# A fused graph and transformer kernel: the written-out order of all queues is redrawn, and the copies of transposed attention weights are shared out evenly between two engines

## The chip, the cores and the metric

The kernel runs on one core of a Trainium2 chip. The metric is device microseconds of one execution. A core has four compute engines with queues of their own (TensorE, called PE in the profile; VectorE, DVE; ScalarE, ACT; GpSimd, POOL) and SyncE (SP), whose queue issues the DMAs here. Each engine takes its instructions strictly in the order of its queue and waits on semaphores for the others.

## The reference

`x` is 16 graphs of 512 nodes with 128 features, `adj` a 512 x 512 integer adjacency for each. Eight blocks are added to `x` one after another, each on a layer norm of what stands before it:

```
x = x + L0_gnn(layernorm(x), adj)   # 3 steps of messages and a GRU cell
x = x + L0_ffn(layernorm(x))        # 8 experts, top 2, gelu
x = x + L1_gnn(layernorm(x), adj)   # graph attention: leaky relu, softmax, elu
x = x + L1_ffn(layernorm(x))        # attention over 64 slices, 8 heads
x = x + L2_gnn(layernorm(x), adj)   # mean of messages
x = x + L2_ffn(layernorm(x))        # Mamba-2 block, chunks of 128
x = x + L3_gnn(layernorm(x), adj)   # two layers of masked attention, 4 heads of 32
x = x + L3_ffn(layernorm(x))        # upper half of tokens through an FFN
```

The part that the change edits is one layer of L3_gnn, for 4 tiles of 128 queries and 4 heads:

```
scores = where(adj > 0, q @ k.T * scale, -1e9)
attn = softmax(scores); out = attn @ v
```

## The kernel before, in words

In the code the eight blocks are g0, f0, g1, f1 (the early half) and g2, f2, g3, f3 (the late half). Matrices are tiled by 128 partitions, T = 4 tiles of 128 nodes. Two graphs are in flight at any time, in two sets of buffers ("lanes"): while graph h goes through its early half, graph h-1 goes through its late half. `halves` (line 396) builds each engine's queue from this: a first phase (graph 0 early, alone), 15 equal periods in which an early and a late half run beside one another, and a last phase (graph 15 late, alone).

Every block is a Python generator that stops at each place where its instructions may be interrupted. A string for each engine (PE_TURNS, ACT_TURNS, DVE_TURNS, POOL_TURNS, SP_TURNS) says whose piece comes next: `e` is the early graph's, `l` the late graph's. The same string serves all 15 periods. PE_FIRST, DVE_FIRST and ACT_FIRST do so for the first phase, PE_LAST for TensorE's last phase; the other engines take their natural order there.

TensorE's strings hold one more kind of turn. A digit (in the periods) or a `w` (in the first and last phase) is a pair of products of the bf16 identity with itself, whose result nobody reads, in a PSUM bank that is free at that point: the "constant products" (`keep`, line 1056, and `keep_bank`, line 1060). They wait for nothing. PE_TURNS of the kernel before has 138 such turns in 28 runs, PE_FIRST has 378, PE_LAST 517.

In g3, each (layer, query tile q, head h), numbered n = 4q + h from 0 to 15 in a layer, goes through this chain:

- TensorE `g3_scores` (line 878): the scores of 4 heads into PSUM.
- VectorE `g3_mask` (line 1860): masks and takes the maximum.
- ScalarE `g3_exp`, then VectorE `g3_sum` (line 1867): exponential and reciprocal of the sum.
- GpSimd `g3_normalise` (line 2089): multiplies by it.
- TensorE `g3_turn` (line 903): four 128 x 128 transposes into PSUM bank 4 (later ones by turns into bank 0); before them it waits until the copy before has emptied the bank.
- `g3_turned`: the copy from PSUM to SBUF. VectorE makes it for head 0 (n % 4 == 0, line 1877), ScalarE for heads 1 to 3.
- TensorE `g3_values`: after 8 of these copies, the product with v.

All of ScalarE's activations are recorded at line 1068, all of TensorE's plain products at line 444, and to_columns (the transposes of a layer-normed tile) at line 453. In stage B below, ScalarE makes the gelu of f0 for the early graph and the exponentials of g3 for the late one; the two functions lie in different activation tables, and a change of table is an ACT_TABLE_LOAD instruction.

Of the kernel before, what the change touches and what calls it, by code (L numbers as in the profile page):

```python
# [28 lines left out]
T = N // P  # L29
# [9 lines left out]
AH, AD = 4, 32  # L39
# [38 lines left out]
    "lleele"  # L78
)
PE_FIRST = (  # L80
    "eewwwwwweeeeeeeeeewwwwwwwwwwwwwwwwwwwwwwwwwwwwwwwwweeeeeeeeeewwwwwwwwwwwwwwwwwwwwwwwwwwwwwwwwweeeeee"
    "eeeewwwwwwwwwwwwwwwwwwwwwwwwwwwwwwwwweppeeeewwwwwwwwweeeeeeeeeeeeeeeeeeeeeeeeeeeeeeeeeeeeeeeeeeeewww"
    "wwwwwwwweeeeewwwwwwwwwwwwwwwwwwwwwwwwwwwwwwwwwwweeeewwwwwweeewwwwwwwwwwwwwwwwwwwwwwwwwwwwwwwwwwweeww"
    "wwwwwewwwwwewwwwwweeeewwwwwwwwwwwwwwwwwwwwwwwwwwwwwwwwwwweeeewwwwwwewwwwewwwwwwwwwwwwwwwwwwweewwwwwe"
    "wwwwwwwwwwwwwwwwwwwwwwewwwwwwweeeeewwwwwwwwwwwwwwwwwwwwwwwwewwwwwwwewwwwwweewwwwwwwwwwwwewwwwwwewwww"
    "wweeee"
# [3 lines left out]
    "wwwwwwwwwlllwwlwlllllllwwwwwwwwwwwwwwwwwwwwwwwwwwwwwwwwwwwlllllllwwwlwwwwwwwwwwwwwwwwwwwwwwwwwllllww"  # L90
    "wwwwwwwwwwwwwwwwwwwwwwwwwwwwwwwwwllllwwwwwwllllwwwwwwwwwwwwwlwwwwwwwwwwwwwwwwwwwwwwwwwwwwllwwwwwwwww"
    "lwwwwwwwwwwwwlllwwwwwwwlwwwwwwwwlwwwwwwwwwwwwlllwwwwwwllllwwwwlwwwwwwwwlwwwwwwwwwwwwllwwwlwwwwwllwwl"
    "wwwwwwllllwllllwwwwwwwwwwwwwlwwwwwwwwwwwwwwwwwwwwwwwwwwwwllwwwwwwwwwlwwwwwwwwwwwwlllwwwwwwwlwwwwwwww"
    "lwwwwwwwwwwwwlllwwwwwwllllwwwwlwwwwwwwwlwwwwwwwwwwwwllwwwlwwwwwllwwlwwwwwwllllwwwllllwwwwwwwwwwwwwww"
    "wwwwwwwwwwwwwwwwwwwwllllwwwwwwllllwwwwwwwl"
# [8 lines left out]
    "ee7777eelellll7777lllllleeeeeeellll7777lllleleeleeeeeellell7lllllll11eeeeeeeeellellll77l7l7777777777"  # L104
    "7e777777777777lllleeee777777eee777777777lleelleelllleeleeee7777leeelleeeeellleleele33333llllllleeeel"
    "eeeeleeeeeeeeeeell44eellelleellll33lleleeeleee7l7777777777777777777eele77e777777leeeel1111lll11111l1"
    "1111111111l11eeeelellellllel111111lellel44ll4lelllleeeeelllle77777e77777ellllelellelelllelee"
)
ACT_TURNS = (
    "eellleeelellllllleellllleleelellleeeeleeeeeelleelllleelllllllllllllleeelelleeleelllllllleleeeeeeelee"  # L110
    "eelleellllllelllllelllelelelellllllelelleleeeeleellll"
)
DVE_TURNS = (
    "ellllelllllllelllleeeeellllllllelllleelllllleelelllllellellelleeelleeeeellleleeleeeeeeleellelllllell"
    "llllellllllllllelleleleellleeeeeeelleeeeellllellllllleeleleleellellleeleeeeleeellellleeelleeeeeeelle"
    "llelleeleellleeeellelle"
)
POOL_TURNS = (
    "llelellellllllllllllllllllellllllleleelllellllleelle"
# [27 lines left out]
def build(nc, x, adj, weights, raw, out):  # L147
# [10 lines left out]
    with ctx:  # L158
# [93 lines left out]
        with nc.Block() as block:  # L252
# [84 lines left out]
            "att_p": 2 * T * AH, "pT_psum": 2 * T * AH, "pT_dve": 2 * T, "pT_act": 2 * T * (AH - 1), "pv_psum": 4, "h3_part": 4,  # L337
# [24 lines left out]
        def turned(layer, n, g):  # L362
            if n % AH == 0:
                return done("pT_dve", g, layer * T + n // AH)
            return done("pT_act", g, (layer * T + n // AH) * (AH - 1) + n % AH - 1)
# [46 lines left out]
        with nc.Block() as block:  # L412
# [29 lines left out]
            def _(pe):  # L442
# [463 lines left out]
                def g3_values(g, layer, pair):  # L906

                    yield
                    pe.wait_ge(*turned(layer, AH * (2 * pair + 1), g))
# [156 lines left out]
            def _(act):  # L1066
# [262 lines left out]
                def g3(g):  # L1329
                    yield from columns_out(g, G3)  # L1330
                    for layer in range(2):
                        yield from g3_project(g, layer)
                        for n in range(T * AH + AH):
                            if n < T * AH:
                                yield from g3_exp(g, layer, n)
                            if n > AH and n % AH:
                                yield from g3_turned(g, layer, n - AH)
# [17 lines left out]
            def _(v):  # L1355
# [636 lines left out]
                def g3(g):  # L1992
                    yield from layernorm(g, G3, X[g])
                    for layer in range(2):
                        yield from g3_project(g, layer)
                        for q in range(T + 1):
# [4 lines left out]
                            if q < T:  # L2001
                                for h in range(1, AH):
                                    yield from g3_mask(g, layer, q * AH + h)
# [211 lines left out]
```

## Time and profile before

| what | value |
|---|---|
| median of 3 runs | 3431.71 us (3428.83 to 3431.92) |
| profiled execution, its own time | 3433.32 us |
| its span in the trace | 3431.5 us |
| mean granted TensorE clock | 0.994 |
| TensorE busy | 3231.9 us, 94% |
| VectorE busy | 2208.7 us, 64% |
| ScalarE busy | 1752.7 us, 51% |
| GpSimd busy | 693.3 us, 20% |

The span is from the first to the last instruction of the trace; the execution's own time also holds what lies around it. Busy time of TensorE counts the constant products as well.

### The profile page before, as it was taken

To read this page: it belongs to the slowest core of one execution; us is meant where nothing else is said; L and a number is where in the kernel's file an instruction comes from. 1 tells how busy PE (TensorE), PEld (TensorE's weight loads), DVE (VectorE), ACT (ScalarE), POOL (GpSimd) and SP (SyncE) were. 2 spreads that over 40 slices of the span, in tenths; PEclk is the share of its full clock that TensorE was granted. 3 is DMA by queue.
4 is the path that set the end of the run, shared out by engine and by line. 5 is a ranking of instruction groups with operands and counts; after the bars stand their busy time and mean duration, and the time that the engine had idled before them with its cause. 6 is when DMAs were issued, how large, how long until landed. Compare 5 with 4: busy or idle time off the path is not lost.

```text
span 3431.5 us, 62674 instructions
## 1 busy us (share of the span) xinstructions
PE 3231.9 (94%) x24744; PEld 2268.1 (66%) x24776; DVE 2208.7 (64%) x7062; ACT 1752.7 (51%) x3195; POOL 693.3 (20%) x804
## 2 busy tenths in 40 slices
PE   8999999999999999999999999999999999999989
PEld 5766666666666666666666666666666666666677
DVE  3476666757567676666757567676666757566653
ACT  2237454563645537454563645537454563645524
POOL 0012122121221212122121221212122121221212
PEclk9999999999999999999999999999999999999999
DMA  3000000000000000000000000000000000000000
GB/s 132 2 7 1 20 4 17 7 1 20 4 17 7 1 22 1 19 4 17 7 1 19 4 17 7 1 22 1 19 4 17 7 1 19 1 4 4 1 8 5
DMA packets 28773, 40.68 MB, mean 12 GB/s; under 512 B 1344, under 2 KB 17728, under 8 KB 28224
## 3 DMA queue, kind: packets, MB, share of 16 engines
q1 hardware_dynamic: 28480, 36.67, 3.4%
q8 instruction: 197, 3.23, 0.4%
q14 instruction: 96, 0.79, 0.1%
HBM read 28.28 MB, written 4.19 MB: 9 GB/s over the span
## 4 chain that ended last, share of the span: by engine, by line
PE 56%; DVE 26%; ACT 11%; issue 5%; POOL 2%; DVEq 0%
PE ps L444 45%; ACT scratch L1068 8%; DVE scratch L1359 5%; PE ps L903 4%; DVE scratch L1362 4%; DVE scratch L1365 3%; DVE scratch L1860 3%; PE ps L453 2%; DVE x L1365 2%; PE ps L1056 2%; DVE stats L1380 2%; POOL rstd L2066 1%; ACT adjf L1068 1%; DVE xn L1362 1%; ACT xT L1068 1%
## 5 line engine op out<-in xcount | busy, mean ns | idle before, releaser
L1068 ACT ACTIVATE scratch<-scratch 128x512 f32<-128x512 f32 (+4 forms) x832 | 564.8, 691 | 278.9 <-DVE scratch L1359 128.9
L444 PE MATMUL ps<-xT,weights_sb 128*128 128x512 f32 x1152 | 560.9, 604 | 7.9 <-ACT xT L1068 7.8
L444 PE MATMUL ps<-scratch 128*128 128x128 f32 (+6 forms) x4608 | 534.4, 379 | 35.7 <-ACT adjf L1068 14.1
L2089 POOL TENSOR_SCALAR scratch<-scratch 128x512 f32<-128x512 f32 x512 | 352.6, 703 | 933.0 <-DVE scratch L1867 932.3
L1068 ACT ACTIVATE scratch<-ps 128x512 f32<-128x512 f32 (+2 forms) x512 | 286.5, 566 | 426.2 <-PE ps L444 230.7
L444 PE MATMUL ps<-weights_sb,scratch 128*128 128x128 f32 (+3 forms) x3840 | 492.6, 278 | 5.9 <-DVE scratch L1503 5.9
L444 PEld LDWEIGHTS ps<-weights_sb,scratch 128*128 128x128 f32 (+3 forms) x3840 | 442.2, 184 | 56.8 <-issue 29.2
L444 PEld LDWEIGHTS ps<-scratch 128*128 128x128 f32 (+5 forms) x4608 | 341.4, 159 | 174.2 <-issue 92.1
L903 PE MATMUL ps<-weights_sb,scratch 128*128 128x128 f32 x2048 | 307.0, 279 | 61.4 <-ACT adjf L1068 24.6
L2066 POOL TENSOR_TENSOR rstd<-ve,minus_half 128x4 f32<-128x4 f32 x126 | 142.9, 1134 | 1081.0 <-DVE ve L1362 1081.0
L1860 DVE CUSTOM_DVE_ANT_0 scratch<-ps,nomask 128x512 f32<-128x512 f32 x512 | 332.7, 683 | 10.5 <-PE ps L444 10.2
L444 PEld LDWEIGHTS ps<-xT,weights_sb 128*128 128x128 f32 x1152 | 197.9, 190 | 212.8 <-issue 145.0
L903 PEld LDWEIGHTS ps<-weights_sb,scratch 128*128 128x128 f32 x2048 | 222.3, 141 | 170.9 <-issue 104.2
L1060 PE MATMUL ps<-ident_bf 128*128 128x128 bf16 x4140 | 300.4, 219 | 0.0
L1068 ACT ACTIVATE scratch<-ps,weights_sb 128x512 f32<-128x512 f32 x368 | 244.8, 686 | 88.5 <-PE ps L444 87.7
L1060 PEld LDWEIGHTS ps<-ident_bf 128*128 128x128 bf16 x4140 | 264.4, 99 | 34.1 <-issue 29.4
L1068 ACT ACTIVATE scratch<-ps,made_sb 128x512 f32<-128x512 f32 x176 | 120.4, 684 | 301.2 <-PE ps L444 301.0
L1068 ACT ACT_TABLE_LOAD x202 | 259.2, 1283 | 18.2 <-PEq L252 14.7
L1068 ACT ACTIVATE xT<-ps 128x512 f32<-128x512 f32 x112 | 66.9, 597 | 342.4 <-PE ps L453 342.4
L444 PE MATMUL ps<-adjf,scratch 128*32 128x256 f32 (+1 forms) x1280 | 241.6, 425 | 0.0
L1365 DVE SCALAR_TENSOR_TENSOR x<-ps,scratch,x 128x128 f32<-128x128 f32 x576 | 161.8, 344 | 111.5 <-PE ps L444 93.6
L1068 ACT ACTIVATE adjf<-ps 128x512 f32<-128x512 f32 (+1 forms) x288 | 166.3, 577 | 89.5 <-PE ps L903 67.2
(166 smaller groups left out, 4520.1 us busy)
## 6 DMA issues: line engine op xcount, KB each, us to landing
adj<-adj SPq DMA_DIRECT2D x16, 1024.0 KB, 5.7
weights_sb<-weights SPq DMA_DIRECT2D x1, 4605.0 KB, 19.0
x_in<-x SPq DMA_DIRECT2D x16, 256.0 KB, 2.8
scratch<-scratch SPq DMA_DIRECT2D x32, 128.0 KB, 2.3
out<-x SPq DMA_DIRECT2D x16, 256.0 KB, 2.4
scratch<-raw SPq DMA_DIRECT2D x1, 1645.0 KB, 22.4
weights_sb<-weights SPq DMA_DIRECT2D x1, 499.0 KB, 6.5
scratch<-raw SPq DMA_DIRECT2D x1, 384.0 KB, 4.9
```

What stands on the lines that cost most here:

```text
L444: return pe.matmul(o, lhsT, rhs, start=start, stop=stop, **k)
L453: last = pe.transpose((ep if k < G2 else lp)(0, P, P, t * P), rows[:, t, 0:D], ident)
L903: last = pe.transpose(lp(turn_bank(n), P, P, j * P), probabilities(g, layer, n)[:, tile(j)], ident)
L1056: pe.matmul(ep(0, P) if h else lp(3, P, P, 384), ident_bf[:, :], ident_bf[:, :], start=True, stop=True)
L1060: pe.matmul(banks[k][0:P, 0:P], ident_bf[:, :], ident_bf[:, :], start=True, stop=True)
L1068: return act.activation(o, a, func, **k)
L1359: return v.tensor_tensor(o, a, c, op)
L1362: return v.tensor_scalar(o, a, s1, s2, op0, op1, **k)
L1365: return v.scalar_tensor_tensor(out=o, in0=a, scalar=s1, in1=c, op0=op0, op1=op1, **k)
L1860: v.tensor_tensor_reduce(probabilities(g, layer, n), lp(n % AH), NM[g][:, n // AH, :], -1.0, 4 * BIG, ALU.add, ALU.min, cut(g, G3_MX + n, ...
L2066: pool.tensor_tensor(rstd[g][:, :], ve[g][:, :], minus_half[:, :], ALU.pow).then_inc(s[f"rstd_ready{g % LANES}"], 1)
L2089: pool.tensor_scalar(p, p, cut(g, G3_RI + n, 1), 1.0, ALU.mult, ALU.mult).then_inc(s["att_p"], 1)
```

## The change

The change has three parts.

1. Who copies. `g3_turned` is made by VectorE for even n (heads 0 and 2) and by ScalarE for odd n (heads 1 and 3). Of the 32 copies of a graph, 8 go from ScalarE to VectorE. In VectorE's queue the new copy of head 2 of tile q - 1 stands after the masks of tile q and before the reciprocals of tile q. `turned` and the semaphore counts follow.
2. The order. PE_TURNS, ACT_TURNS, DVE_TURNS, POOL_TURNS and SP_TURNS are new strings.
3. The constant products. PE_TURNS has 124 turns of them in 26 runs, PE_FIRST 376, PE_LAST 537.

The edits of the code:

```diff
         def turned(layer, n, g):
-            if n % AH == 0:
-                return done("pT_dve", g, layer * T + n // AH)
-            return done("pT_act", g, (layer * T + n // AH) * (AH - 1) + n % AH - 1)
+            return done("pT_act" if n % 2 else "pT_dve", g, (layer * T * AH + n) // 2)
...
                 def g3_values(g, layer, pair):
                     yield
-                    pe.wait_ge(*turned(layer, AH * (2 * pair + 1), g))
+                    pe.wait_ge(*turned(layer, AH * (2 * pair + 2) - 2, g))
                     pe.wait_ge(*turned(layer, AH * (2 * pair + 2) - 1, g))
...
# ScalarE's g3
-                            if n > AH and n % AH:
+                            if n > AH and n % 2:
                                 yield from g3_turned(g, layer, n - AH)
...
# VectorE's g3
                             if q < T:
                                 for h in range(1, AH):
                                     yield from g3_mask(g, layer, q * AH + h)
+                            if q:
+                                yield from g3_turned(g, layer, (q - 1) * AH + 2)
+                            if q < T:
                                 for p in range(2 * q, 2 * q + 2):
                                     yield from g3_sum(g, layer, p)
```

The new order of TensorE and SyncE (VectorE's, ScalarE's and GpSimd's strings are redrawn in the same way):

```diff
 SP_TURNS = (
-    "lleele"
+    "elleel"
 PE_TURNS = (
-    "ee7777eelellll7777lllllleeeeeeellll7777lllleleeleeeeeellell7lllllll11eeeeeeeeellellll77l7l7777777777"
-    "7e777777777777lllleeee777777eee777777777lleelleelllleeleeee7777leeelleeeeellleleele33333llllllleeeel"
-    "eeeeleeeeeeeeeeell44eellelleellll33lleleeleeee7l7777777777777777777eele77e777777leeeel1111lll11111l1"
-    "1111111111l11eeeelellellllel111111lellel44ll4lelllleeeeelllle77777e77777ellllelellelelllelee"
+    "ele7777ee77777llllelllllleeeeeeellll7777llllelleeeeeelelllellllelll222222eeeeelllellllleeeelllle7777"
+    "7777777777777777777777777777777777eeeellllelllleel7eeeeeeeeel7eleeeeeeeleeeeeeeleeeeelleeeleeeleelll"
+    "eeelllleleleeleel4llll66666llleeeeleeelllelee7l7e7777e7l7leeel33333ll222l22222l22222l333333333ll2l22"
+    "222lllle3leee333lelelll6666lleellllelllle77777eeeellllelleleleellle77777eleeee"
```

## Rows read from the trace of the kernel before

The stages of the period from 1207.3 to 1413.1 us are: A, to 1281.4 (g0 beside g2 and f2); B, to 1331.0 (f0 beside layer 0 of g3); C, to 1384.0 (g1 and the start of f1 beside layer 1 of g3); D, to 1413.1 (the end of f1 beside f3).

**Rows 1.** The page: busy us of the engines; group of the constant products.
```profile
...
PE 3231.9 (94%) x24744; PEld 2268.1 (66%) x24776; DVE 2208.7 (64%) x7062; ACT 1752.7 (51%) x3195; POOL 693.3 (20%) x804
...
L1060 PE MATMUL ps<-ident_bf 128*128 128x128 bf16 x4140 | 300.4, 219 | 0.0
...
```

**Rows 2.** Windows (first phase, a period, last): us, busy PE PEld DVE ACT POOL, clock.
```profile
...
0.00:178.00 178.00, 161.38 (x1328) 121.67 (x1331) 77.82 (x244) 42.85 (x70) 13.51 (x16) 0.92 0.17 64
1207.30:1413.10 205.80, 194.74 (x1448) 134.97 (x1450) 137.22 (x440) 109.88 (x200) 43.46 (x50) 1.00 0.04 10
3265.40:3431.50 166.10, 149.91 (x1698) 122.27 (x1698) 77.61 (x260) 62.86 (x126) 29.88 (x40) 0.96 0.02 6
...
```

**Rows 3.** Timeline of SyncE's queue: start, duration, the stores of the output.
```profile
...
383.84 0.39 SPq L434 DMA_DIRECT2D out<-x  x1
...
3265.43 0.39 SPq L434 DMA_DIRECT2D out<-x  x1
...
```

**Rows 4.** The page's chain that ended last, by engine.
```profile
...
PE 56%; DVE 26%; ACT 11%; issue 5%; POOL 2%; DVEq 0%
...
```

**Rows 5.** Windows over one period cut into stages A to D.
```profile
...
1207.30:1281.40 74.10, 70.85 (x436) 45.21 (x437) 58.25 (x166) 31.54 (x47) 10.71 (x8) 1.00 0.09 26
1281.40:1331.00 49.60, 46.82 (x352) 33.40 (x355) 25.20 (x84) 37.18 (x67) 10.85 (x16) 1.00 0.00 1
1331.00:1384.00 53.00, 48.59 (x431) 33.73 (x423) 34.62 (x110) 33.98 (x76) 18.61 (x23) 1.00 0.01 2
1384.00:1413.10 29.10, 28.48 (x241) 22.64 (x239) 19.15 (x82) 7.18 (x11) 3.30 (x3) 1.00 0.01 1
...
```

**Rows 6.** The same windows, the constant products (L1060) alone.
```profile
...
1207.30:1281.40 74.10, 8.05 (x112) 7.37 (x112) 1.00 0.09 26
1281.40:1331.00 49.60, 1.72 (x22) 1.48 (x22) 1.00 0.00 1
1331.00:1384.00 53.00, 8.79 (x122) 7.66 (x122) 1.00 0.01 2
1384.00:1413.10 29.10, 1.46 (x20) 1.12 (x20) 1.00 0.01 1
...
```

**Rows 7.** Timeline of TensorE in stage C: start, duration, idle before it and releaser.
```profile
...
1342.22 2.29 PE L1060 MATMUL ps<-ident_bf 128*128 128x128 bf16 x38
...
1359.44 1.39 PE L1060 MATMUL ps<-ident_bf 128*128 128x128 bf16 x22
1361.11 0.63 PE L903 MATMUL ps<-weights_sb,scratch 128*128 128x128 f32 x4 [0.28 <-DVE scratch L1877]
...
```

**Rows 8.** Timeline of TensorE in the last phase.
```profile
...
3307.59 4.07 PE L1056 MATMUL ps<-ident_bf 128*128 128x128 bf16 x70
...
```

**Rows 9.** Waits of TensorE in one period: total us, times, longest.
```profile
...
PE ps L903 <- ACT adjf L1068: 1.6, 5, 0.4
PE ps L903 <- DVE scratch L1877: 1.4, 3, 0.9
...
```

**Rows 10.** Groups by line and form, ScalarE in stage B.
```profile
...
L1068 ACT ACT_TABLE_LOAD x7 | 9.0, 1283 | 0.1
...
L1068 ACT ACTIVATE adjf<-ps 128x512 f32<-128x512 f32 x8 | 4.7, 588 | 2.5 <-PE ps L903 2.5
...
```

**Rows 11.** Groups by line, ScalarE over the whole period: the table loads.
```profile
...
L1068 ACT ACT_TABLE_LOAD x13 | 16.7, 1283 | 0.2
...
```

**Rows 12.** Timeline of ScalarE around one table load.
```profile
...
1288.51 1.28 ACT L1068 ACT_TABLE_LOAD   x1
1289.81 0.72 ACT L1068 ACTIVATE scratch<-scratch 128x512 f32<-128x512 f32 x1
...
```

**Rows 13.** Groups by line, VectorE in stage B: the copies.
```profile
...
L1877 DVE COPY scratch<-ps 128x512 f32<-128x512 f32 x4 | 2.8, 691 | 8.9 <-PE ps L903 8.9
...
```

**Rows 14.** Windows where the granted clock was not full.
```profile
...
56.00:77.00 21.00, 21.00 (x110) 15.72 (x108) 6.16 (x22) 3.43 (x4) 1.01 (x1) 0.67 0.19 63
3295.40:3307.40 12.00, 10.41 (x73) 8.49 (x71) 7.15 (x26) 5.01 (x8) 0.74 (x1) 0.72 0.10 22
...
```

More of the change, by code:

```diff
@@ L77 @@
 SP_TURNS = (
-    "lleele"
+    "elleel"
 )
 PE_FIRST = (
[L81 to L86, printed above, removed]
+    "eewwwwwweeeeeeeeeewwwwwwwwwwwwwwwwwwwwwwwwwwwwwwwweeeeeeeeeewwwwwwwwwwwwwwwwwwwwwwwwwwwwwwwweeeeeeee"
+    "eewwwwwwwwwwwwwwwwwwwwwwwwwwwwwwwweppeeeewwwwwwwwweeeeeeeeeeeeeeeeeeeeeeeeeeeeeeeeeeeeeeeeeeeewwwwww"
+    "wwwwweeeeewwwwwwwwwwwwwwwwwwwwwwwwwwwwwwwwwwweeeewwwwwwweeewwwwwwwwwwwwwwwwwwwwwwwwwwwwwwwwwwweewwww"
+    "wwwewwwwwewwwwwweeeewwwwwwwwwwwwwwwwwwwwwwwwwwwwwwwwwwweeeewwwwwwewwwwewwwwwwwwwwwwwwwwwwweewwwwweww"
+    "wwwwwwwwwwwwwwwwwwwwewwwwwwweeeeewwwwwwwwwwwwwwwwwwwwwwwwewwwwwwwewwwwwweewwwwwwwwwwwwewwwwwwewwwwww"
+    "eeee"
 )
@@ L89 @@
     "lllllwwwwwwllllllwwwwwwwwwwwwwwwwwwwwwwwwwwwwwwwwwwwllllwwwwwwllllwwwwwwllwwwwwwwwwwwwwwwwwwwwwwwwww"
[L90 to L95, printed above, removed]
+    "wwwwwwwwwlllwwlwlllllllwwwwwwwwwwwwwwwwwwwwwwwwwwwwwwwwwwwlllwwwwwlwwwwwwwwlllwwlwwwwwwwwwwwwwwwwwww"
+    "wwwwwwllllwwwwwwwwwwwwwwwwwwwwwwwwwwwwwwwwwwwllllwwwwwwllllwwwwwwwwwwwwwlwwwwwwwwwwwwwwwwwwwwwwwwwww"
+    "wllwwwwwwwwwlwwwwwwwwwwwwlllwwwwwwwlwwwwwwwwlwwwwwwwwwwwwlllwwwwwwllllwwwwlwwwwwwwwlwwwwwwwwwwwwllww"
+    "wwwwwwwwwwllwwllwwwwwwllllwllllwwwwwwwwwwwwwlwwwwwwwwwwwwwwwwwwwwwwwwwwwwllwwwwwwwwwlwwwwwwwwwwwwlll"
+    "wwwwwwwlwwwwwwwwlwwwwwwwwwwwwlllwwwwwwllllwwwwlwwwwwwwwlwwwwwwwwwwwwllwwwwwwwwwwwwllwwllwwwwwwllllww"
+    "wllllwwwwwwwwwwwwwwwwwwwwwwwwwwwwwwwwwwwllllwwwwwwllllwwwwwwwl"
 )
@@ L103 @@
 PE_TURNS = (
-    "ee7777eelellll7777lllllleeeeeeellll7777lllleleeleeeeeellell7lllllll11eeeeeeeeellellll77l7l7777777777"
-    "7e777777777777lllleeee777777eee777777777lleelleelllleeleeee7777leeelleeeeellleleele33333llllllleeeel"
-    "eeeeleeeeeeeeeeell44eellelleellll33lleleeeleee7l7777777777777777777eele77e777777leeeel1111lll11111l1"
-    "1111111111l11eeeelellellllel111111lellel44ll4lelllleeeeelllle77777e77777ellllelellelelllelee"
+    "ele7777ee77777llllelllllleeeeeeellll7777llllelleeeeeelelllellllelll222222eeeeelllellllleeeelllle7777"
+    "7777777777777777777777777777777777eeeellllelllleel7eeeeeeeeel7eleeeeeeeleeeeeeeleeeeelleeeleeeleelll"
+    "eeelllleleleeleel4llll66666llleeeeleeelllelee7l7e7777e7l7leeel33333ll222l22222l22222l333333333ll2l22"
+    "222lllle3leee333lelelll6666lleellllelllle77777eeeellllelleleleellle77777eleeee"
 )
 ACT_TURNS = (
-    "eellleeelellllllleellllleleelellleeeeleeeeeelleelllleelllllllllllllleeelelleeleelllllllleleeeeeeelee"
-    "eelleellllllelllllelllelelelellllllelelleleeeeleellll"
+    "eelleleelelllllleellllllleeellelleeleeeleeeleelllleeeelleeleellelelllllleellllllllleleeeeeeeeeleeeel"
+    "lllllllelllllllllelllllelelleleeeeellelleleee"
 )
 DVE_TURNS = (
-    "ellllelllllllelllleeeeellllllllelllleelllllleelelllllellellelleeelleeeeellleleeleeeeeeleellelllllell"
-    "llllellllllllllelleleleellleeeeeeelleeeeellllellllllleeleleleellellleeleeeeleeellellleeelleeeeeeelle"
-    "llelleeleellleeeellelle"
+    "lllleelllllllellleleeeelllllllllellllllllelellleeelllllllllelleeeeeleeleellleleeeeeeeeelllelelelllel"
+    "lllleelelllllelllllleellellllleleeeleeeeeeelllllllellllllelleellllllleelellelllleelleleeeleleeeeeeee"
+    "elllllleeellelelleleeeeeeelelee"
 )
 POOL_TURNS = (
-    "llelellellllllllllllllllllellllllleleelllellllleelle"
+    "lllellelelllllllllllllllllellllllllellllelllleeeelle"
 )
@@ L336, in build @@
             "qkv_psum": 2, "q_ready": 2, "kv_ready": 2, "att_psum": 2 * T, "att_max": 2 * T * AH, "att_exp": T * AH, "att_rsum": T * AH,
-            "att_p": 2 * T * AH, "pT_psum": 2 * T * AH, "pT_dve": 2 * T, "pT_act": 2 * T * (AH - 1), "pv_psum": 4, "h3_part": 4,
+            "att_p": 2 * T * AH, "pT_psum": 2 * T * AH, "pT_dve": T * AH, "pT_act": T * AH, "pv_psum": 4, "h3_part": 4,
             "g3_psum": 1,
```

## Prediction

> **What bounds the kernel now.** I read the page's busy times first: TensorE is busy 94% of the span [rows 1]. That number holds the constant products too, so it does not yet say that TensorE is at its limit. Then the windows and SyncE's queue: the stores of the output stand 3265.43 - 383.84 = 2881.6 us apart over 14 periods [rows 3], 205.8 us each, at full clock; the first phase has 178 us and the last 166 us [rows 2]. Fifteen periods are 3087 us, nine tenths of the span, so whatever the change does to one period counts 15 times.
>
> Inside a period TensorE is busy 194.7 of 205.8 us [rows 2]. Of this 20.0 us are 276 constant products, 112 + 22 + 122 + 20 [rows 6], which is 138 turns of two. So 174.7 us are products that the answer needs, and 31 us are waits, two thirds of which are filled. The chain that ended last says the same from the other side: 56% TensorE, 26% VectorE, 11% ScalarE [rows 4]. No single engine sets the end; the hand-overs between them do, and the order decides how much of one graph's hand-overs lies under the other graph's products.
>
> The reader should now see what the constant products are: a ruler. In the trace a run of them ends just before the product behind it can start. A run of 22 starts at 1359.44 and lasts 1.39 us, and the transposes behind it wait another 0.28 us for VectorE's copy [rows 7]. So the length of a run is, nearly, the wait that it covers. I therefore read the new string of TensorE as a statement of how long its waits will be, and check that statement against the other engines' work.
>
> **The change, part by part.**
>
> *The price of one turn.* The run of 38 at 1342.22 takes 2.29 us, of which 0.22 us is the length of the last product itself [rows 1]; the other 37 starts stand 0.056 us apart. The run of 70 in the last phase, 4.07 us, gives the same [rows 7, 8]. A turn is two products: 0.112 us.
>
> *Periods: turns of constant products.* By stages, from the order of the pieces in the two strings: A had 56 turns and has 57, B had 11 and has 8, C and D together had 71 and have 59. That is 138 to 124. Fourteen turns are 14 x 0.112 = 1.57 us of a period, 23.5 us over 15. This is the main term. It counts as a gain only if the waits are really shorter, not if fewer are filled. Two things speak for it. The number of runs also falls, from 28 to 26, so the unfilled rests behind runs (0.28 us in the row) do not grow in number. And 12 of the 14 turns vanish in C and D, where layer 1 of g3 has its transposes and copies.
>
> *Periods: the copies.* Eight of 32 copies leave ScalarE, at 0.588 us each [rows 10], 4.7 us of ScalarE's time in a period, and come to VectorE at 0.691 us [rows 13], 5.5 us. VectorE is busy 25.2 of 49.6 us in B and 34.6 of 53.0 in C [rows 5], so it has room: its busy share in C goes from 65% to some 70%. Its copies do not wait behind its own work today but for TensorE, 8.9 us in B for 4 of them [rows 13]. From the other side: TensorE waited 1.4 us for VectorE's 8 copies and 1.6 us for ScalarE's 24 in a period [rows 9], 0.18 us a copy against 0.07. Eight more copies on VectorE could thus cost 8 x 0.11 = 0.9 us of a period. Bounds of this part: a gain of 4.7 us if every copy taken from ScalarE had been bare, a loss of 0.9 us. I take it as already inside the 1.57 us, which lies between them.
>
> *Periods: activation tables.* This is what the new order of ScalarE costs. In B the order alternates between gelu for the early graph and exp for the late one, and each change is a table load. The trace shows 7 loads in B [rows 10] and 13 in a period [rows 11]. Counting the changes in the new string: B goes exp, gelu, exp, gelu, exp, gelu, exp, gelu, exp after its first gelu, 9 loads. At the period's end f1's exp now follows f3's gelus and needs a load, but it spares the one that f2's softplus needed. So 15 loads, 2 more: 2 x 1.283 = 2.57 us of ScalarE in a period. ScalarE is busy 37.2 of 49.6 us in B [rows 5]. Its B account is 4 copies less (2.4 us) and 2 loads more (2.6 us), so +0.2 us: the relief that the copies bring there is spent. In C there is no such cost. Bounds: nothing if each load falls into a wait of ScalarE, 2.57 us a period if both stand bare. I take nothing for the forecast, because 12.4 us of B are left idle on ScalarE, and keep 2.57 for the range.
>
> A load costs what the row says: it starts at 1288.51, lasts 1.28 us, and the next activation starts at 1289.81, 1.30 us after it [rows 12]. The Trainium skill ("ScalarE: Activation LUTs", section "What ACT_TABLE_LOAD costs") puts about 1380 ns of drain on top, 2.66 us for every switch. By that figure the two loads would be an estimated 5.3 us of a period; the trace does not show the drain, and the sum goes by 1.283.
>
> *Periods: the rest of the order.* In A both lanes now reach their layer norms together: f2's output products stand before g0's last transposes, and one run of 38 turns (4.3 us) covers both, where four runs of 11, 12, 6 and 9 turns stood before, 38 as well. That is neutral. SyncE's new string puts the load of the next adjacency ahead of the store of the output. It waits there for the cast on GpSimd, which is early in the period, and the store is needed by nobody in the period; GpSimd is busy 43.5 of 205.8 us [rows 2]. Both cost nothing; if the store came late by its own 2 to 3 us it would show only behind the last graph, where nothing stands in front of it.
>
> *First and last phase.* PE_FIRST has 2 turns fewer: -0.2 us. PE_LAST has 20 more: 12 around f2's states, 8 in the two layers of g3. At 0.112 us that is +2.2 us if they stand on the path, 0 if they fill waits. I take +2.2, as the last phase runs alone and has nothing to hide them.
>
> *The sum.* -23.5 - 0.2 + 2.2 = -21.5 us. On the span: 3431.5 - 21.5 = 3410.0; the profiled execution's own time, 3433.3, is 1.8 above its span and 1.6 above the median of the runs, so the median comes to 3431.7 - 21.5 = **3410 us**, 0.63% faster.
>
> **The rivals.**
>
> *Table loads in front of the gelus (slower).* The place is B: each gelu pair of experts 2 to 7 waits for an exp pair and a load, and f0's output products wait for the gelu. If both new loads stand bare, the period changes by -1.57 + 2.57 = +1.0 us, 15 us in all, plus 2 for the tail: 3431.7 + 15 - 0.2 + 2.2 = 3449 us. It decides from 1.57 of the 2.57 us bare. For it: TensorE has only 1.7 us of constant products in B [rows 6], so its filled slack there is thin. Against it: TensorE has work of both graphs there and ScalarE's idle 12 us. By the figure of the Trainium skill ("ScalarE: Activation LUTs", the same section) both bare would be an estimated +3.7 us a period, some 3490 us in all; the row on the load [rows 12] speaks against it.
>
> *A wash (same).* The copies wait on VectorE as they do now (0.9 us) and half a load is bare (0.64 us): 1.54 against 1.57 us of gain. That leaves the tail: 3433 us. For it: VectorE holds its queue in order, and the copy of head 2 stands behind three masks of 0.7 us each.
>
> *The clock falls (slower).* At 3295.4 to 3307.4 the mean granted clock was 0.72, and at 56 to 77 it was 0.67 [rows 14]: between the two levels of 1.2 and 2.4 GHz, 0.72 means 2 x 0.28 x 12 = 6.7 us at the low one, in which 3.4 us are lost where TensorE is the limit. TensorE was busy only 10.4 of the 12 us of the former [rows 14], in short pieces with waits between them. If the new order makes such a stretch in each period, that is 15 x 3.4 = 50 us: 3410 + 50 = 3460 us. Against it: the longest wait is filled by the run of 38, and the period before is at full clock throughout [rows 5].
>
> *More than the ruler says (faster).* The two runs fewer save their rests as well, 2 x 0.28 us, and a quarter of the 4.7 us of copies turns out bare beyond it: 1.7 us a period more, 3384 us.
>
> **How the numbers follow.** About 0.2%, 7 us, is what a measurement of this kernel can tell from no change. Forecast 0.55, more than it 0.07: the faster side has 0.62, with a little of the wash rival's spread 0.64. Wash 0.15. Table loads 0.13 and clock 0.08: 0.21. The likeliest case has 3400 to 3420 as its own range (the 0.56 us of rests either way). The range for 8 in 10 reaches to the table rival and half-way to the upper gain: 3392 to 3449.
>
> **What would show it.** In the profile after: a period (distance of two output stores) of some 204.2 us; 248 constant products and 15 table loads in it; 8 + 8 copies by line 1877 in a period and 16 by ScalarE; TensorE's waits for VectorE's copies up, by less than 1 us a period; a granted clock of 1.00 in every window of a period. Wrong would be the reading of the ruler if the period is not shorter although 28 products are gone: then TensorE's idle time would have grown by as much, and the windows by stage would say where. If B alone is longer, it was the loads; if A has a window under full clock, it was the clock; if the last phase is not longer, its 20 turns filled waits.

## The result, and the profile after

The kernel after takes 3339.61 us (median of 4 runs, 3338.1 to 3343.2) against 3431.64 us for the kernel before on the same chip: ratio 0.9735, 95% interval 0.9718 to 0.9752. The forecast was 3410, its range 3392 to 3449. The direction was right, the gain is 92 us where 21.5 were forecast, and the time lies under the range.

The profiled execution took 3338.16 us, its span is 3336.3 us. Line numbers shift a little: L1060 is L1058 now, L1877 is L1875, L2089 is L2090, L444 is L442, L903 is L901. From the page, the busy times and three groups:

```profile
PE 3171.5 (95%) x24375; PEld 2236.2 (67%) x24392; DVE 2293.5 (69%) x7190; ACT 1732.0 (52%) x3097; POOL 684.4 (21%) x804
...
L1066 ACT ACT_TABLE_LOAD x232 | 297.7, 1283 | 18.3 <-PEq L252 14.2
...
L1058 PE MATMUL ps<-ident_bf 128*128 128x128 bf16 x3720 | 272.3, 219 | 0.0
...
L1875 DVE COPY scratch<-ps 128x512 f32<-128x512 f32 x256 | 175.5, 685 | 100.4 <-PE ps L901 98.7
```

The counts are those foretold: 3720 / 15 = 248 constant products and 256 / 16 = 16 copies by VectorE. The table loads rose by 30 over 15 periods, 2 in each. Now the windows of the first phase, one period and the last phase (length in us, busy us of PE, PEld, DVE, ACT, POOL, then the granted clock, the share of time in which the DMA engines are busy, and GB/s), which answer to [rows 2]:

```profile
0.00:178.00 178.00, 160.53 (x1364) 119.38 (x1367) 82.03 (x258) 44.64 (x73) 15.43 (x17) 0.97 0.17 64
1167.70:1367.40 199.70, 190.81 (x1423) 132.94 (x1424) 142.47 (x448) 108.83 (x194) 42.84 (x51) 1.00 0.03 10
3164.00:3336.30 172.30, 156.31 (x1753) 127.98 (x1751) 82.95 (x268) 56.86 (x117) 29.75 (x40) 0.95 0.02 6
```

And two stores of the output in SyncE's queue, the first and the last but one, which answer to [rows 3]:

```profile
369.03 0.39 SPq L432 DMA_DIRECT2D out<-x  x1
...
3163.95 0.38 SPq L432 DMA_DIRECT2D out<-x  x1
```

They are 14 periods apart: 199.64 us each, against 205.8 before. The reader should see that this one number explains the result: 15 x 6.19 = 93 us, and the medians are 92 us apart. The two profiled spans differ by 95.2; the other 2 to 3 us are the two ends, a first phase of 170.2 instead of 177.8 us (up to g0's first transposes of the second graph) and a last one (from the end of the early half's last product) of some 170.5 instead of 166.1.

Where in the period? For this I cut both traces at the same pieces of TensorE's work: A from g0's first transposes, B from f0's first transposes, C from the first value product of g3's layer 0, second pair, D from the same of layer 1. (These cuts differ from those of [rows 5]: they are pieces of work, so they mean the same in every kernel below.) The kernel before:

```profile
1207.34:1272.97 65.63, 62.75 (x382) 40.28 (x383) 51.24 (x136) 27.20 (x40) 8.59 (x6) 1.00 0.10 29
1272.97:1329.73 56.76, 53.66 (x383) 37.48 (x381) 31.03 (x109) 41.51 (x73) 12.97 (x18) 1.00 0.00 1
1329.73:1380.61 50.88, 46.47 (x404) 31.94 (x406) 35.76 (x114) 32.53 (x74) 17.65 (x23) 1.00 0.01 1
1380.61:1413.12 32.51, 31.87 (x285) 25.27 (x285) 19.17 (x82) 8.63 (x14) 4.26 (x4) 1.00 0.01 2
```

The kernel after:

```profile
1168.51:1235.97 67.46, 62.90 (x416) 41.78 (x415) 52.27 (x153) 25.59 (x39) 8.89 (x8) 1.00 0.08 23
1235.97:1288.52 52.55, 51.52 (x344) 35.08 (x345) 33.97 (x112) 42.68 (x71) 12.24 (x18) 1.00 0.02 8
1288.52:1334.71 46.19, 43.34 (x372) 29.80 (x373) 34.27 (x99) 29.09 (x66) 15.27 (x20) 1.00 0.01 1
1334.71:1368.24 33.53, 33.09 (x294) 26.30 (x293) 21.99 (x86) 11.47 (x18) 6.47 (x6) 1.00 0.00 1
```

A and B together give 2.4 us (32 constant products more stand in A and 36 fewer in B, so neither should be read alone), C gives 4.7, and D takes back 1.0. What makes C shorter is seen on VectorE. Its timeline around the start of C, before (start, duration, then the idle time before it and who ended it):

```profile
1329.83 1.13 DVE L1365 SCALAR_TENSOR_TENSOR x<-ps,scratch,x 128x128 f32<-128x128 f32 x4 [1.55 <-PE ps L444]
...
1333.63 1.12 DVE L1362 TENSOR_SCALAR xn<-x,mv,rstd 128x128 f32<-128x128 f32 x4 [1.14 <-POOL rstd L2066]
1339.04 0.69 DVE L1538 CUSTOM_DVE_ANT_0 scratch<-ps,nomask 128x512 f32<-128x512 f32 x1 [4.30 <-PE ps L444]
```

And after:

```profile
1284.30 1.12 DVE L1363 SCALAR_TENSOR_TENSOR x<-ps,scratch,x 128x128 f32<-128x128 f32 x4
...
1288.94 1.11 DVE L1360 TENSOR_SCALAR xn<-x,mv,rstd 128x128 f32<-128x128 f32 x4 [0.55 <-POOL rstd L2067]
1292.46 0.69 DVE L1536 CUSTOM_DVE_ANT_0 scratch<-ps,nomask 128x512 f32<-128x512 f32 x1 [2.41 <-PE ps L442]
```

The first line is the last combine of f0, the second writes g1's normalized input, the third is g1's first masked score. Against the start of C, the combine stood at +0.1 us and stands at -4.2; the score stood at +9.3 us and stands at +3.9. Two edits do this. f0's last expert goes ahead of the last transposes of layer 0, so the layer norm between f0 and g1 runs under them. And g1's transposes and projection go ahead of layer 1's projection, which before was what filled the layer norm's wait. Then VectorE's four masked scores and ScalarE's exponentials lie under that projection, where before TensorE waited for them in the run of 38 [rows 7]. ScalarE's row that opens g1's leaky relus and exponentials, before and then after:

```profile
1341.32 3.16 ACT L1068 ACTIVATE scratch<-scratch 128x512 f32<-128x512 f32 x5
```

```profile
1294.74 3.16 ACT L1066 ACTIVATE scratch<-scratch 128x512 f32<-128x512 f32 x5
```

g1's next transposes on TensorE start at 1344.62 before, right behind the run of 38, and at 1298.37 after, between two products of layer 1's projection.

### The profile page after: what moved, and what is told of

It reads as the page before. It is cut to its first block, busy times and chain, and to the rows that moved or that the text cites. A ratio compares the mean times of both kernels' runs of the same rounds, so it can differ in the third digit from the quotient of the medians.

```text
span 3336.3 us, 61964 instructions
## 1 busy us (share of the span) xinstructions
PE 3171.5 (95%) x24375; PEld 2236.2 (67%) x24392; DVE 2293.5 (69%) x7190; ACT 1732.0 (52%) x3097; POOL 684.4 (21%) x804
## 2 busy tenths in 40 slices
DMA packets 28770, 40.63 MB, mean 12 GB/s; under 512 B 1344, under 2 KB 17728, under 8 KB 28224
## 4 chain that ended last, share of the span: by engine, by line
PE 67%; DVE 22%; ACT 5%; issue 3%; POOL 3%; DVEq 0%
PE ps L442 53%; PE ps L901 5%; ACT scratch L1066 4%; DVE scratch L1357 3%; DVE scratch L1360 3%; PE ps L451 3%; POOL rstd L2067 2%; DVE scratch L1363 2%; DVE stats L1378 2%; PE ps L1054 2%; DVE xn L1360 2%; DVE scratch L1875 2%; DVE scratch L1858 1%; PE ps L614 1%; DVE mv L1383 1%
## 5 line engine op out<-in xcount | busy, mean ns | idle before, releaser
L442 PE MATMUL ps<-xT,weights_sb 128*128 128x512 f32 x1152 | 564.3, 601 | 7.3 <-ACT xT L1066 7.2
L2090 POOL TENSOR_SCALAR scratch<-scratch 128x512 f32<-128x512 f32 x512 | 357.7, 719 | 1014.9 <-DVE scratch L1865 1013.2
L442 PE MATMUL ps<-scratch 128*128 128x128 f32 (+6 forms) x4608 | 527.5, 378 | 19.5 <-DVE scratch L1357 4.6
L442 PE MATMUL ps<-weights_sb,scratch 128*128 128x128 f32 (+3 forms) x3840 | 485.2, 278 | 24.6 <-ACT adjf L1066 21.6
L442 PEld LDWEIGHTS ps<-weights_sb,scratch 128*128 128x128 f32 (+3 forms) x3840 | 438.8, 183 | 82.2 <-issue 43.4
L442 PEld LDWEIGHTS ps<-scratch 128*128 128x128 f32 (+5 forms) x4608 | 334.7, 159 | 141.0 <-issue 67.3
L1066 ACT ACTIVATE scratch<-ps 128x512 f32<-128x512 f32 (+2 forms) x384 | 212.7, 562 | 315.6 <-PE ps L442 197.5
L901 PE MATMUL ps<-weights_sb,scratch 128*128 128x128 f32 x2048 | 313.0, 278 | 34.0 <-ACT adjf L1066 14.9
L901 PEld LDWEIGHTS ps<-weights_sb,scratch 128*128 128x128 f32 x2048 | 224.8, 141 | 139.9 <-issue 83.2
L1066 ACT ACT_TABLE_LOAD x232 | 297.7, 1283 | 18.3 <-PEq L252 14.2
L442 PEld LDWEIGHTS ps<-xT,weights_sb 128*128 128x128 f32 x1152 | 196.0, 191 | 152.4 <-issue 126.6
L1058 PEld LDWEIGHTS ps<-ident_bf 128*128 128x128 bf16 x3720 | 235.6, 98 | 80.1 <-issue 76.8
L1058 PE MATMUL ps<-ident_bf 128*128 128x128 bf16 x3720 | 272.3, 219 | 0.0
L1875 DVE COPY scratch<-ps 128x512 f32<-128x512 f32 x256 | 175.5, 685 | 100.4 <-PE ps L901 98.7
L442 PE MATMUL ps<-adjf,scratch 128*32 128x256 f32 (+1 forms) x1280 | 243.9, 425 | 0.0
```

The source lines that it names most:

```text
L442: return pe.matmul(o, lhsT, rhs, start=start, stop=stop, **k)
L901: last = pe.transpose(lp(turn_bank(n), P, P, j * P), probabilities(g, layer, n)[:, tile(j)], ident)
L1058: pe.matmul(banks[k][0:P, 0:P], ident_bf[:, :], ident_bf[:, :], start=True, stop=True)
L1066: return act.activation(o, a, func, **k)
L1875: v.tensor_copy(pt[:, :, tile(n // AH % 2)], lp(turn_bank(n)).rearrange("p (j n) -> p j n", j=T)).then_inc(s["pT_dve"], 1)
L2090: pool.tensor_scalar(p, p, cut(g, G3_RI + n, 1), 1.0, ALU.mult, ALU.mult).then_inc(s["att_p"], 1)
```

## The experiments

Fifteen kernels ran. The strings of turns are long, so a diff shows the piece that differs. "Period" is the mean of the 14 distances between the first 15 output stores of the profiled run. In the kernel after the first 12 of them lie between 199.70 and 199.75 us; the total also holds the two end phases, at a changing clock.

| kernel | period us | median us | ratio to before (95%) |
|---|---|---|---|
| before | 205.8 | 3431.6 | |
| after | 199.6 | 3339.6 | 0.9735 (0.9718 to 0.9752) |
| new_order_old_split | 199.7 | 3342.3 | 0.9739 (0.9710 to 0.9767) |
| old_order_even_split | 215.2 | 3576.5 | 1.0421 (1.0380 to 1.0462) |
| new_order_late_stages | 211.2 | 3511.8 | 1.0232 (1.0202 to 1.0262) |
| new_order_early_stages | 208.2 | 3467.9 | 1.0104 (1.0075 to 1.0134) |
| late_stages_old_split | 207.2 | 3454.6 | 1.0067 (1.0044 to 1.0090) |
| early_stages_old_split | 203.2 | 3393.2 | 0.9891 (0.9863 to 0.9920) |
| early_opening | 202.1 | 3374.4 | 0.9832 (0.9802 to 0.9862) |
| early_turns | 200.4 | 3350.2 | 0.9758 (0.9738 to 0.9777) |
| late_opening | 206.4 | 3445.0 | 1.0032 (1.0019 to 1.0046) |
| before_no_constant | 210.2 | 3501.7 | 1.0208 (1.0178 to 1.0237) |
| after_no_constant | 204.2 | 3412.6 | 0.9944 (0.9922 to 0.9967) |
| before_half_constant | 206.7 | 3443.1 | 1.0025 (1.0013 to 1.0037) |
| before_tanh | 205.8 | 3430.6 | 1.0000 (0.9988 to 1.0011) |
| after_tanh | 199.5 | 3339.5 | 0.9730 (0.9702 to 0.9759) |
| after_first_last | 199.6 | 3338.4 | 0.9726 (0.9709 to 0.9742) |

Two slips in the expectations: they put the turns of constant products of the kernel before at 131 (262 products) and of the halved one at 72, where the counts are 138 (276) and 75; and the 124 turns of the kernel after took 18.2 us a period, not 23.

### The order or the split

```diff
# old_order_even_split, against the kernel after
 PE_TURNS = (
-    "ele7777ee77777llllelllllleeeeeeellll7777llllelle...
+    "ee7777eelellll7777lllllleeeeeeellll7777lllleleel...
# new_order_old_split, against the kernel before
 PE_TURNS = (
-    "ee7777eelellll7777lllllleeeeeeellll7777lllleleel...
+    "ele7777ee77777llllelllllleeeeeeellll7777llllelle...
```

> The kernel after, with the five turn strings of a period taken back to the order of before (the four copies per layer that the new split gives to VectorE are put in behind VectorE's masks, those taken from ScalarE left out); first and last phase as after. The 262 constant products per period of before are back. If the order of the turns made the gain, the period stays at 205.8 us, within 1.5, and the run near 3430 us. If the even split made it (ScalarE freed of 8 copies, PE waiting less for them), the period falls towards 200 us and the run to about 3345. If both are needed, the period is at or over 205.8 here and the other run of this pair is slow too.

> The kernel before with all turn strings of the kernel after, the split of the copies left at one in four by VectorE (VectorE's extra turns left out, ScalarE's copies put back behind the exponentials that they followed before). If the order made the gain, the period is 199.6 to 201.5 us and the run 3340 to 3370. If the split made it, the period is 204 to 206 us and the run over 3400.

The new order with the old split has the whole gain: 199.7 us. The split by itself, in this place of the new order, is worth nothing that can be measured. In the old order it costs 9.4 us a period (some 8.1 in the two of its 14 periods that ran at a full clock, 213.9 us each), and the waits of TensorE (total us over the span, times, longest) say how:

```profile
PE ps L901 <- POOL scratch L2090: 67.2, 60, 2.7
PE ps L442 <- DVE scratch L1501: 28.0, 16, 1.9
PE ps L442 <- DVE scratch L1875: 27.3, 15, 1.8
```

TensorE waits for GpSimd's weights, 67 us where the same view of the kernel before has 16.0. GpSimd in its turn waits for VectorE's reciprocals for 1036 us where it waited 932. A likely reading, argued and not tested alone, is that VectorE's added copies stand behind three masks in a queue that was not drawn for them, so that the reciprocals behind them come late. Only this one placement of the copies was tried in the old order. In the new order the same view has TensorE waiting for VectorE's copies for 13.0 us with the even split (9.7 at L901, 3.3 at L442) and 16.7 us with the old one, for ScalarE's at those lines for 39.8 and 51.4 us; the period did not notice either.

### Which stage

```diff
# late_stages_old_split, against the kernel before: new from the start of C on
-    "eeeeleeeeeeeeeeell44eellelleellll33lleleeeleee7l7777777777777777777eele77e777777l...
+    "eeeeleeeeeeeeeeell44eellelleellleeeeleeelllelee7l7e7777e7l7leeel33333ll222l22222l...
# early_stages_old_split keeps the new strings up to there and the old ones behind
```

> The kernel before (one copy in four by VectorE) with the new order only from g1's start to the end of the period (stages C and D). Stages independent: C and D give 3.7 to 4.2 us, so a period of 201.6 to 202.1 us. If the new C needs the new B ahead of it, the period is 205 or more.

> The kernel before with the new order only up to g1's start (stages A and B). Stages independent: A and B give 1.8 to 2.4 us, so a period of 203.4 to 204 us. If the old C cannot use what B gives, 205.8 or more.

The early half gives 2.6 us, a little more than the stage lengths said. The late half alone loses 1.4 us. Together they give 6.2: 4.9 us belong to neither but to the pair. Part of this is the clock, as the windows of C show, first in the kernel with the late half new, then in the one with the early half new:

```profile
1329.80:1380.39 50.59, 45.00 (x373) 30.95 (x372) 34.27 (x108) 31.17 (x70) 16.47 (x21) 0.97 0.01 1
```

```profile
1313.36:1364.26 50.90, 46.73 (x405) 32.04 (x406) 33.20 (x101) 32.55 (x74) 17.11 (x23) 1.00 0.01 1
```

With the early half new, C is as long as it was (50.9 us). f0's last combine stands 3.8 us ahead of the start of C there, nearly as in the kernel after, but g1's first masked score stays at +9.3 us, and VectorE is idle for 7.69 us before it instead of 4.30:

```profile
1322.67 0.69 DVE L1538 CUSTOM_DVE_ANT_0 scratch<-ps,nomask 128x512 f32<-128x512 f32 x1 [7.69 <-PE ps L444]
```

So the earlier end of f0 alone is worth nothing to the old C, in which g1 still opens behind layer 1's projection. With the new C behind the old B, g1's transposes have nothing in front of them and TensorE stands for the layer norm:

```profile
1334.09 1.10 PE L453 MATMUL ps<-weights_sb,xn 128*128 128x128 f32 x4 [2.79 <-DVE xn L1362]
```

```profile
1334.10:1340.10 6.00, 5.88 (x29) 3.89 (x30) 1.41 (x5) 0.98 (x2) 0.00 (x0) 0.72 0.01 3
```

Behind that wait the granted clock is 0.72 for 6 us: some 2 x 0.28 x 6 = 3.4 us at the lower of the two levels, in which TensorE is almost always busy, an estimated 1.7 us lost. The period says the same. It is 207.2 us in the mean, but one of the 14 ran at a full clock, with the same wait of 2.8 us in it:

```profile
2242.99:2448.51 205.52, 192.86 (x1428) 133.97 (x1427) 139.06 (x439) 110.12 (x200) 44.05 (x51) 1.00 0.04 10
```

So at a full clock the late half alone gains 0.3 us, and 3.2 of the 4.9 us belong to the pair of orders; the rest goes with the clock behind the bare wait.

The same two halves were run on the kernel with the even split, from the base of 215.2 us:

> The kernel after with the new order only from g1's start to the end of the period (stages C and D of the table by stage); stages A and B in the old order, with the even split. By the stage lengths of the two traces (C 50.9 to 46.2 us, D 32.5 to 33.5) the period is 3.7 us under that of the old order with the even split, about 202. If the stages are not independent (what C gives is given back at the next A), it is within 1 us of it.

> The kernel after with the new order only up to g1's start (stages A and B), C and D in the old order. By the stage lengths (A and B together 122.5 to 120.1 us) the period is 2.5 us under that of the old order with the even split, about 203.3; with the run of the late stages the two savings add up to the 6.2 us between the two kernels, if the stages are independent.

There they gave 4.0 and 7.0 us of 15.6: both missed their numbers, which were worked out from stage lengths that belong to a base of 205.8. These runs are disturbed by the clock too (0.978 to 0.987 over the run). In their periods at a full clock the base takes 213.9 us, the late half 207.9 and the early half 207.2, so they gain 6.0 and 6.7 of the 14.2 us to the kernel after. From this base the two halves come near to adding up, and only 1.5 us are left to the pair.

### The opening of g1

```diff
# late_opening, against the kernel after (PE_TURNS; ScalarE's and VectorE's strings likewise)
-    "...66666llleeeeleeelllelee7l7e7777e7l7leeel33333...
+    "...66666lllllleleeeleeeeee7l7e7777e7l7leeel33333...
```

> The kernel after with the start of stage C put back to what it was: PE finishes all four value products of g3's layer 0 and issues layer 1's projection before g1's transposes are done and before g1's own projection; ScalarE and VectorE serve g3's projection before g1's. Nothing else is moved. If the 4.7 us of stage C come from g1 opening ahead of that projection, the period grows from 199.6 to between 203 and 205 us (the projection's products take about 3.4 us on PE). If they come from the rest of C's order, it stays within 1 us.

The period goes to 206.4 us, over the 203 to 205 expected; all 6.8 us are in C, more than the 3.4 us of products that were swapped. Timeline of TensorE, then windows (clock is the third number from the end):

```profile
1344.40 0.90 PE L582 MATMUL ps<-weights_sb,scratch 128*128 128x128 f32 x3 [3.83 <-ACT scratch L1066]
```

```profile
1334.50:1340.50 6.00, 6.00 (x41) 4.75 (x39) 1.68 (x4) 1.28 (x2) 0.00 (x0) 1.00 0.00 0
1340.50:1346.50 6.00, 2.04 (x9) 1.57 (x8) 2.50 (x10) 5.40 (x11) 0.00 (x0) 0.74 0.00 0
1346.50:1352.50 6.00, 5.35 (x35) 3.41 (x36) 2.18 (x7) 3.67 (x10) 0.00 (x0) 0.69 0.01 3
```

The wait of 3.83 us is bare here, since the new string has no run of constant products in that place, and the granted clock falls from 1.00 to 0.74 and 0.69 in the two windows that hold the wait (1340.6 to 1344.4) and what follows. In them some 2 x 0.26 x 6 + 2 x 0.31 x 6 = 6.8 us are at the lower level; cut into windows of 1 us, the clock reads 0.50 from 1344 to 1350. Eight score products of g3 take 2.09 us there and 1.14 us at 1352.9, at full clock. TensorE is busy for some 5.4 of the 6.8 us, so the clock costs an estimated 2.7 us of the period and the late opening itself the other 4.

The other direction, from early_stages_old_split:

```diff
# early_opening, against early_stages_old_split (PE_TURNS)
-    "...66666llll33lleleeeleee7l7777777777777777777eele77e777777l...
+    "...66666llleeeeleeellll7l77eele77e777777l...
# early_turns, against early_opening (PE_TURNS)
-    "...66666llleeeeleeellll7l77eele77e777777l...
+    "...66666llleeeeleeelllelee7l7e7777l7l...
```

> The kernel early_stages_old_split (new order up to g1's start, old behind it, period 203.2 us) with g1 opened ahead of layer 1's projection on PE, ScalarE and VectorE, and 19 turns of constant products fewer (the run of 19 at 1342.22 us of the kernel before cut to 2, 2 more at the opening dropped). If opening g1 early is what shortens C, the period falls to 198.5 to 200.5 us. If it takes the whole new order of C, it stays over 202.

> The kernel early_opening carried one step on: also g1's four transposes of its weights (g1_turn) and ScalarE's copies of them stand where the new order has them, inside and just behind layer 1's projection; the rest of stages C and D in the old order; 113 turns of constant products a period. early_opening showed two waits of 1.4 us each behind the projection (at 1320.62 and 1324.40 us), which these transposes could fill. If they are the missing piece, the period falls from 202.1 to 199.3 to 200.5 us. If what is missing lies further on (layer 1's own turns and f1), it stays over 201.3.

The opening alone gave 1.1 us: the expectation of 198.5 to 200.5 failed, and the other branch, over 202, came true. Two waits had come in its place:

```profile
1320.62 1.14 PE L444 MATMUL ps<-scratch 32*128 32x512 f32 x8 [1.42 <-DVE scratch L1359]
...
1324.40 1.14 PE L444 MATMUL ps<-scratch 32*128 32x512 f32 x8 [1.44 <-DVE scratch L1860]
```

With g1's four transposes (g1_turn, its copies on ScalarE ahead of layer 1's exponentials) moved into them, the period is 200.4 us, within its expectation. So the account of the 6.2 us, taken in this sequence, is: 2.6 for A and B, 1.1 for g1 ahead of the projection, 1.8 for its transposes inside it, 0.7 for all the rest of C and D. Taken in another sequence the parts come out otherwise, as the late half alone shows. Both steps also took out constant products, 19 and 4 turns. What in A and B makes their 2.6 us no run takes apart, and none moves f0's last expert alone.

### The constant products

```diff
# after_no_constant and before_no_constant: every digit taken out of PE_TURNS
# before_half_constant: each run of digits cut to half
-    "ee7777eelellll7777lllllleeeeeeellll7777l...
+    "ee77eelellll77lllllleeeeeeellll77l...
```

> The kernel after without the 124 turns of constant products in a period (first and last phase keep theirs); no output depends on them. If every turn lies in a wait and the clock stays at 1.00, the period stays at 199.6 us and the waits grow by the 23 us that the turns took. If the turns are longer than the waits (the runs push the needed products back), the period falls, by 1 to 4 us. If the clock falls in the bare waits, as it did at 56 to 77 us of the kernel before, the period grows: needed products behind a wait at half the clock take about twice as long, and 8 to 10 waits with 5 to 10 us of such products behind each give 10 to 40 us.

> The kernel before without its 131 turns of constant products in a period. The forecast took the length of the runs of constant products as the length of the waits that the order leaves. If that holds, this run and its twin differ by what the two kernels differ, 6 us a period; and both periods stay if the clock does. If the turns of before were partly too many and those of after are not, the period of before falls towards 200 us here and the two orders come out alike.

> The kernel before with each run of constant products in a period cut to half (131 turns become 72). If the length of a run is a measure of the wait it stands in (the forecast's ruler), the kernel does not notice (each wait goes on as long, bare), and the period stays at 205.8 us as long as the clock does; if runs push products back, it falls by up to the 6 us taken out; if the clock falls with them, it grows towards the 210.2 us of the kernel with none.

Two periods of the halved kernel:

```profile
385.14:590.93 205.79, 187.69 (x1322) 127.89 (x1325) 137.19 (x440) 109.87 (x200) 43.46 (x50) 1.00 0.04 10
590.93:798.08 207.15, 189.12 (x1323) 128.50 (x1325) 137.20 (x440) 109.89 (x200) 43.47 (x50) 0.99 0.03 10
```

The first is as long as a period before (205.8) with 126 constant products fewer: TensorE is busy 7.0 us less and idle 7.0 us more. The second is 1.4 us longer and at a clock of 0.99. Five of the 14 periods of this kernel take 205.8 us, at a clock of 1.00; the others take up to 208.2 us, at a clock down to 0.98, and the mean is 206.7. So the half that was taken out lay in waits entirely, and is worth the clock that it holds. How many constant products an order has can then differ by half with the same waits. Without any, both kernels lose about 4.5 us, at a clock near 0.96 (first the kernel before, then after):

```profile
1441.71:1651.78 210.07, 183.57 (x1175) 123.17 (x1175) 137.31 (x440) 109.87 (x200) 43.46 (x50) 0.97 0.03 10
```

```profile
1194.86:1399.66 204.80, 183.29 (x1176) 121.74 (x1175) 142.60 (x448) 108.66 (x194) 42.82 (x50) 0.96 0.03 10
```

Their periods are 210.2 and 204.2 us: the two orders stand 6.0 us apart with no constant product in either. The gain is not in them, though at this clock the two are not compared at full speed.

### The table loads

```diff
# before_tanh and after_tanh
-                        f(cut(g, F0_HID + (2 * (e % 2) + k) * N, N), ep(k), ACT.Gelu,
+                        f(cut(g, F0_HID + (2 * (e % 2) + k) * N, N), ep(k), ACT.Tanh,
```

> The kernel before with Tanh in place of Gelu in f0's hidden layer, so that the function is one of the table that the exponentials use and most of the table loads of stage B go (13 a period become about 6). It computes another function there. If the loads lie bare in front of PE's products, each is worth up to 1.28 us and the period falls by up to 9 us; if they lie in ScalarE's slack, by under 1 us.

> The kernel after with the same replacement (Tanh for Gelu in f0's hidden layer; 15 table loads a period become about 6). The forecast held the two more loads a period for free. If they are, after and before fall by the same amount within 0.5 us and stay 6 us apart; if the two loads are paid for elsewhere in the gain, after falls by up to 2.6 us more than before.

The page's group in the changed kernel before (the one of after has the same count and time):

```profile
L1068 ACT ACT_TABLE_LOAD x80 | 102.6, 1283 | 16.3 <-PEq L252 14.9
```

In the kernel before 122 loads, 156 us of ScalarE, are gone, and the period is 205.8 as it was. In the kernel after 152 are gone and it is 0.2 us shorter. So the loads of B, the two that the new order adds among them, cost nothing that the period shows. (These two kernels compute another function in f0.)

### First and last phase

```diff
# after_first_last, against the kernel after: PE_FIRST and PE_LAST of the kernel before
-    "eewwwwwweeeeeeeeewwwwwwwwwwwwwwwwwwwwwwwwwwwwwwwweeeeeeeeewww...
+    "eewwwwwweeeeeeeeewwwwwwwwwwwwwwwwwwwwwwwwwwwwwwwwweeeeeeeeeewww...
```

> The kernel after with the first and last strings of PE (PE_FIRST, PE_LAST) of the kernel before: 2 turns of constant products more in the first phase, 20 fewer in the last. If the shorter first phase (177.8 to 170.2 us) came from the new string, the first period starts at 177 to 178 us here; if it was the clock's draw in one execution, it may start at either, and the median moves by less than 5 us from 3339.6. If the 20 turns lengthened the last phase (163.4 to 169.6 us between the last two stores), it is 4 to 6 us shorter here.

The median is 3338.4 us, 1.2 under after and within what a run scatters. With the old string the first period starts at 170.4 us, and in new_order_old_split, which has the new string, at 176.7: the 7.6 us are not the string's. The windows of that stretch, after and then new_order_old_split, show what differs:

```profile
60.00:120.00 60.00, 57.62 (x469) 45.25 (x468) 29.99 (x101) 22.30 (x38) 1.01 (x1) 0.94 0.04 16
```

```profile
60.00:120.00 60.00, 57.83 (x391) 44.96 (x391) 29.14 (x99) 15.82 (x24) 2.01 (x2) 0.86 0.07 23
```

It is the clock, 0.94 against 0.86, which comes out differently from one execution to another. The last two stores are 169.0 us apart with the old string and 169.6 with the new one, so the 20 turns do not lengthen the last phase by more than 0.7. Over all runs that distance lies between 163.3 us (before) and 169.8; why it is at its long end in the kernel after stays open.

## Why the prediction was wrong, and where it was right

The prediction said itself that the hand-overs set the end and that the order decides how much of them is covered. It then priced the order by its filler. The step that failed is **"the turns of constant products" as the main term**, with its premise that "the length of a run is, nearly, the wait that it covers". The term was -1.57 us a period, -23.5 in all; the order's real share is -6.2 us, -92 in all. The row behind the premise was read rightly: a run does end 0.28 us before its wait does [rows 7]. What does not follow is that the sum over runs moves with the sum over waits. Halving the runs left the period at 205.8 us as long as the clock was full (206.7 in the mean), and taking them all out left the two orders 6.0 us apart. Even their own busy time fell by only 1.9 us of the 6.1 us between the windows (20.0 [rows 6] to 18.2, with the same mean of 219 ns); TensorE's idle time fell by 2.2 (11.1 to 8.9), and the busy time of the products that the answer needs by 2.0 (174.7 to 172.7). The last is probably that fewer of them stand first behind a wait, where nothing overlaps them; that is argued, not shown.

The sign of error that it gave, a period not shorter although 28 products are gone, was no test of this: it looked only for runs that overstate the gain.

The prediction should have followed the hand-overs instead. All that the mechanism needs stood in the trace of before: f0's combine, the layer norm and the first score of g1, and 4.30 us of VectorE's idle time before that score. The strings of the change told that g1 now opens ahead of layer 1's projection.

- **The rest of the order taken as neutral.** Wrong for C. A was rightly called neutral: it is 1.8 us longer and has 32 constant products more, 32 x 0.056 = 1.8 us, which B gave up (36 fewer there). B was put at 3 turns, 0.3 us, and gives 2.4 with A; C and D were put at 12 turns, 1.3 us, and give 3.7.
- **The copies**, taken as inside the term with bounds of +4.7 and -0.9 us: their effect in the new order is 0.1 us a period at most, between the bounds. The wait for VectorE's copies fell from 20.3 to 13.0 us over the span instead of rising. Its price of 0.07 us for a copy of ScalarE counted only the waits in front of the transposes; those in front of the products with v (L444 and then L442, for `adjf`) were 14.1 us over the span before and are 24.9 after.
- **The table loads**, counted as 2 more a period and held for free: right on both, count (202 to 232) and cost. By the Trainium skill ("ScalarE: Activation LUTs", section "What ACT_TABLE_LOAD costs") each switch would also carry about 1380 ns of drain, 2.66 us with the load; if all of it were on the path, taking out 8 loads a period would have shortened it by an estimated 21 us. The runs show 0.0 and 0.2 us.
- **SyncE and GpSimd at nothing**: no run sets this apart; early_turns, with the new SyncE string replaced by the old one, comes within 0.7 us of after, which leaves little room.
- **The first phase** at -0.2 and **the last** at +2.2 us: together 1.2 us by the medians, in the noise; the 20 turns measured 0.7 us at most.
- **The rivals.** The slower ones did not come: the clock is 1.00 in all four stages of the period after. The one called "more than the ruler says" was the right side, at 3384 us and a chance of 0.07, for the wrong reason: bare copies and rests behind runs, which would be 1.7 us more. The clock rival's mechanism is real, as late_opening and late_stages_old_split show, but this order does not set it off.
- **The range** was built on the bounds of the copies and loads. It had no bound for the order itself, the largest part of the change. From the rows of before, the 31 us of waits a period, filled or not, are such a bound; 4 of them went (20.0 + 11.1 to 18.2 + 8.9). Its lower end was also not where it was said to be: half-way from 3410 to 3384 is 3397, not 3392.

## What to carry to other kernels

When an order of work is redrawn, don't read filler as a measure of the waits; take the longest chain from one stage to the next of each lane (here combine, layer norm, transposes, projection, scores) and ask what each order puts over it. A piece of an order has no price of its own: the late half cost 1.4 us alone (and gained 0.3 in a period at full clock) and was worth 3.5 us behind the new early half, and the split that was free in one order cost 9.4 us in the other. Read the granted clock beside each part, since a bare wait that a partial order leaves can lower it and pass for a cost of the order. Time such parts by the period, cut at the same pieces of work, since the phases at the ends of a run scatter by more than the parts are worth.

## What was not expected of the hardware

Taking 122 table loads out of ScalarE, 156 us of its time, in a stage where it is busy 41.5 of 56.8 us, changed nothing, though its activations are handed to TensorE all along. And one bare wait of 3.83 us, in a period that is else at full clock, lies in 12 us with a granted clock of 0.74 and 0.69; two waits of 1.42 and 1.44 us in early_opening are followed by no window below 1.00; and the same wait of 2.8 us in late_stages_old_split is there in a period at a clock of 1.00 (205.5 us) and in one at 0.98 (208.4 us).
